# Letting ScalarE load one tile of neighbour rows per pass, row by row, in a graph kernel whose gathers run on GpSimd

## The reference, cut to what matters

```
def _rgcn_layer(x, W, SW, b, src, dst, rel):
    xt = jnp.einsum('nd,rde->rne', x, W)
    agg = jax.ops.segment_sum(xt[rel, src], dst, num_segments=x.shape[0])
    return jax.nn.relu(agg + x @ SW + b)
...
x1 = rgcn(x, w1, sl1, b1);  x2 = rgcn(x1, w2, sl2, b2);  x = layernorm(x + x2)
feat = jax.nn.relu(x @ W1 + b1)
h = feat * d_invsqrt
agg = jax.ops.segment_sum(h[src], dst, num_segments=N)
out = layernorm(x + (feat - agg * d_invsqrt) @ W2 + b2)
```

## Time and profile before

| | |
|---|---|
| time, median of 3 runs | 6150.97 us (6150.61 to 6153.27) |
| the profiled execution's own time | 6150.52 us |
| its span, first to last instruction | 6148.7 us |
| GpSimd busy | 4639.2 us (75%) |
| TensorE busy | 3443.3 us (56%) |
| VectorE busy | 1587.8 us (26%) |
| ScalarE busy | 475.0 us (8%) |

### The profile page before, as it was taken

The page is one execution under the profiler, slowest core; times in us unless marked ns, Lnnn a source line. Parts: engine busy times, 40 slices in busy tenths (PEclk is TensorE's granted clock), DMA queues, the critical chain, the costliest instruction groups (busy, mean ns, idle before and its releaser), DMA issues.

```text
span 6148.7 us, 76649 instructions
## 1 busy us (share of the span) xinstructions
PE 3443.3 (56%) x13474; PEld 2442.4 (40%) x13626; DVE 1587.8 (26%) x2521; ACT 475.0 (8%) x1056; POOL 4639.2 (75%) x4906
## 2 busy tenths in 40 slices
PE   4666666666666666666666666674434434344344
PEld 3343333433344444344343434353333333333333
DVE  5433333433344222122221222231111111111111
ACT  1000000000010111011110101010000000000000
POOL 7777777777777777777777777777777777777776
PEclk8776776777676767777667676775555555555555
DMA  2222222222222222222222222222222222121222
GB/s 78 63 58 61 64 58 61 57 64 61 57 61 63 60 64 67 67 67 61 74 60 67 67 65 69 68 66 59 60 57 60 60 60 60 57 64 56 60 60 60
DMA packets 220298, 384.36 MB, mean 63 GB/s; under 512 B 96977, under 2 KB 117196, under 8 KB 220108
## 3 DMA queue, kind: packets, MB, share of 16 engines
q0 software_dynamic: 156672, 321.18, 18.3%
q1 hardware_dynamic: 61766, 60.62, 3.1%
q10 hardware_dynamic: 1670, 0.85, 0.0%
HBM read 356.54 MB, written 25.73 MB: 62 GB/s over the span
## 4 chain that ended last, share of the span: by engine, by line
POOL 72%; issue 25%; PE 2%; POOLq 0%; DVE 0%; DMA 0%; ACT 0%; DVEq 0%; ACTq 0%; SPq 0%
POOL rows L804 72%; PE bank L961 1%; PE bank L989 1%; POOL rows L786 0%; POOLq L812 0%; POOLq L797 0%; DMA rows<-in_x_dram,idx 0%; DVE acc L1071 0%; PE bank L1382 0%; POOLq L106 0%; PE bank L1303 0%; ACT r_agg L924 0%; PE bank L1511 0%; DMA rows<-h_d,idx 0%; PE bank L1296 0%
## 5 line engine op out<-in xcount | busy, mean ns | idle before, releaser
L804 POOL DMA_INDIRECT rows<-in_x_dram,idx x1632 | 1545.9, 947 | 499.9 <-issue 496.5
L804 POOL DMA_INDIRECT rows<-h_d,idx x1611 | 1531.1, 950 | 491.2 <-issue 490.9
L804 POOL DMA_INDIRECT rows<-x_d,idx x1618 | 1527.9, 944 | 493.5 <-issue 493.5
L989 PE MATMUL bank<-r_S,rows 128*128 128x128 f32 x6644 | 1230.3, 359 | 972.6 <-DMA rows<-x_d,idx 453.2
L989 PEld LDWEIGHTS bank<-r_S,rows 128*128 128x128 f32 x6644 | 1155.4, 266 | 1052.2 <-issue 1040.1
L1164 PE MATMUL bank<-r_S,rows 128*128 128x64 f32 x3322 | 767.7, 424 | 1138.7 <-DMA rows<-h_d,idx 1122.7
L1164 PEld LDWEIGHTS bank<-r_S,rows 128*128 128x128 f32 x3322 | 726.2, 331 | 1182.7 <-DMA rows<-h_d,idx 674.0
L1027 DVE TENSOR_TENSOR r_S<-bank,key 128x1792 f32<-128x1792 f32 x238 | 480.3, 2018 | 932.2 <-PE bank L989 927.3
L924 ACT COPY r_agg<-bank 128x512 f32<-128x512 f32 x476 | 278.5, 585 | 2491.3 <-PE bank L989 2472.7
L1208 DVE TENSOR_TENSOR acc<-acc,bank 128x64 f32 x238 | 52.8, 222 | 1613.3 <-PE bank L1164 1597.5
L961 PE MATMUL bank<-r_agg,w1s 128*128 128x512 f32 (+1 forms) x512 | 447.7, 1043 | 25.9 <-ACT r_agg L924 25.9
(11 more groups left out here) (157 smaller groups left out, 1317.8 us busy)
## 6 DMA issues: line engine op xcount, KB each, us to landing
rows<-in_x_dram SPq DMA_DIRECT2D x3712, 0.5 KB
rows<-x_d SPq DMA_DIRECT2D x3712, 0.5 KB
rows<-h_d SPq DMA_DIRECT2D x3712, 0.5 KB
rows<-in_x_dram,idx POOLq DMA_INDIRECT x1632, 2.5
rows<-x_d,idx POOLq DMA_INDIRECT x1618, 2.5
rows<-h_d,idx POOLq DMA_INDIRECT x1611, 2.5
d_xr<-in_x_dram SPq DMA_DIRECT2D x48, 256.0 KB, 2.9
x_d<-d_yr SPq DMA_DIRECT2D x24, 256.0 KB, 3.1
```

The source lines that it names most:

```text
L804: pool.indirect_dma_start(out=self.c.rows[:, self.place(s), :], out_offset=None, in_=self.table[:, :], in_offset=bass.IndirectOffsetOnAxis ...
L989: mm = pe.matmul(agg_ps[j][:, bass.ds(offs[j * KG + k], TK)], c.rows[:, g.place(h * KG + k), :], S[:, pb, j * KG + k, :], start=False, sto ...
```

## The change

A second tile of every full pass leaves GpSimd, which gathers 54: `OWN = (UN - 2, UN - 1)`. Both own tiles are the last of group 7; SyncE now loads tile 54 (`BY_SYNC`), ScalarE tile 55 (`BY_ACT`). ScalarE loads its tile with the same `load_own`, in eight lists of 16 rows: three at once at the end of a pass (`own_next`, behind the last copy and `take`, ahead of the chunk's tail), one at the start of the next pass ahead of the first copy, and one behind each of the copies of groups 0 to 3 (in layer 3: two behind each of the first two `take`s). It fetches its next list of addresses after the eighth. At the start of a layer `own_first` issues the first three lists ahead of the tail's first `d_xT`. Semaphores are shared (`node_src_out`, `lo_hi_rel_out`, `yzf_turned`, `zf_copied`, `fv_mm` and others), which makes room for the new ones; the waits stay, with other counts.

```
-OWN = UN - 1
+OWN = (UN - 2, UN - 1)
+BY_SYNC, BY_ACT = range(2)
 LIST = 16
+LISTS = P // LIST
+AT_ONCE = 3
+assert LISTS == AT_ONCE + 1 + 4
...
-                        if s < skip or (part is FULL and s == OWN):
+                        if s < skip or (part is FULL and s in OWN):
                             continue
...
+    def fetch_list(self, eng, o, i):
+        eng.dma_start(self.c.list_i[o][0:1, :], self.c.own_d[bass.ds(i, 1), o, :]).then_inc(self.list_in[o], 16)
+    def own_free(self, eng, o, q, i):
+        eng.wait_ge(self.summed, self.pairs_summed(q, i, OWN[o] // PT))
+        self.list_there(eng, o, q, i)
+        gate(eng, self.c.passed)
+    def load_own(self, nc, eng, o, lists):
+        for first in [n * LIST for n in lists]:
+            _, starts = nc.values_load_multi_w_load_instructions(
+                c.list_i[o][0:1, first:first + LIST], engines=bass.OrderedEngineSet([eng.engine]), ...)
+            for row, start in enumerate(starts, first):
+                eng.dma_start(to[row:row + 1, :], table[bass.ds(start, ROW)].unsqueeze(0)
+                              ).then_inc(self.own[o][row // (P // OWN_SEMS)], 16)
...
 # layers 1 and 2, ScalarE
         with act.Fori(0, rounds) as q:
+            own_first(nc, act, c, g, q)
             def iteration(i, part):
+                if part is FULL:
+                    g.load_own(nc, act, BY_ACT, [AT_ONCE])
                 act.wait_ge(mixed, q * NIT + i + 1)
                 for h in range(...):
                     act.wait_ge(summed, ...)
                     act.copy(agg[:, h, :, :], ...)
                     if part is FULL and h % PAIR == PAIR - 1:
                         g.take(act, h // PAIR, q, i + 1)
+                    if part is FULL and AT_ONCE + 1 + h < LISTS:
+                        g.load_own(nc, act, BY_ACT, [AT_ONCE + 1 + h])
+                        if AT_ONCE + 2 + h == LISTS:
+                            g.fetch_list(act, BY_ACT, i + 1)
+                if part is FULL:
+                    own_next(nc, act, g, q, i)
             by_chunk(act, c, q, iteration, tail.act_early, tail.act_late)
...
+def own_first(nc, act, c, g, q):
+    act.wait_ge(g.cleared, q + 1)
+    gate(act, c.passed)
+    g.fetch_list(act, BY_ACT, 0)
+    g.own_free(act, BY_ACT, q, 0)
+    g.load_own(nc, act, BY_ACT, range(AT_ONCE))
+def own_next(nc, act, g, q, i):
+    with act.If(i < IT - 1):
+        g.own_free(act, BY_ACT, q, i + 1)
+        g.load_own(nc, act, BY_ACT, range(AT_ONCE))
+    act.end_ifs()
...
 # layer 3, ScalarE
                 if part is FULL:
+                    g.load_own(nc, act, BY_ACT, [AT_ONCE])
                     for p in range(PR):
                         g.take(act, p, q, i + 1)
+                        if p < PR // 2:
+                            g.load_own(nc, act, BY_ACT, [AT_ONCE + 1 + 2 * p, AT_ONCE + 2 + 2 * p])
+                        if p == PR // 2 - 1:
+                            g.fetch_list(act, BY_ACT, i + 1)
+                    own_next(nc, act, g, q, i)
```

More of the change, by code:

```diff
@@ L150, in build @@
         c.gs8 = sb("gs8", [1, NG])
-        c.list_i = sb("list_i", [1, P], I32)
+        c.list_i = [sb(f"list_i{o}", [1, P], I32) for o in range(len(OWN))]
         c.step_t, c.step_g, c.carry = sb("step_t", [P, 1]), sb("step_g", [P, 1]), sb("carry", [P, 1])
@@ L730, in __init__ @@
         assert [s.num - self.landed[0].num for s in self.landed] == list(range(RING + PAIR))
-        self.own = [sem(f"own{b}") for b in range(OWN_SEMS)]
-        assert [s.num - self.landed[-1].num for s in self.own] == list(range(1, OWN_SEMS + 1))
-        self.list_in = sem("list_in")
+        self.own = [[sem(f"own{o}_{b}") for b in range(OWN_SEMS)] for o in range(len(OWN))]
+        assert [s.num - self.landed[-1].num for own in self.own for s in own] == list(range(1, len(OWN) * OWN_SEMS + 1))
+        self.list_in = [sem(f"list_in{o}") for o in range(len(OWN))]
         self.cleared = sem("cleared")
@@ L829, in run @@
                 pool.dma_reset(landed)
-                pool.sem_clear(range(self.landed[0].num, self.own[-1].num + 1))
+                pool.sem_clear(range(self.landed[0].num, self.own[-1][-1].num + 1))
                 pool.sem_inc(self.cleared, 1)
@@ L835, in run @@
             self.early(pool, rounds, stored)
-    def load_own(self, nc, sync, q, i):
-        c = self.c
[L840 to L844, removed]
-        for first in range(0, P, LIST):
+    def fetch_list(self, eng, o, i):
+        eng.dma_start(self.c.list_i[o][0:1, :], self.c.own_d[bass.ds(i, 1), o, :]).then_inc(self.list_in[o], 16)
@@ new lines, in own_free, with list_there @@
+    def own_free(self, eng, o, q, i):
+        eng.wait_ge(self.summed, self.pairs_summed(q, i, OWN[o] // PT))
+        self.list_there(eng, o, q, i)
+        gate(eng, self.c.passed)
+    def list_there(self, eng, o, q, i):
+        eng.wait_ge(self.list_in[o], q * ((IT + o) * 16) + i * 16 + 16)
+    def load_own(self, nc, eng, o, lists):
+        c = self.c
+        to, table = c.rows[:, self.place(OWN[o]), :].bitcast(U8), self.table.bitcast(U8).rearrange("n b -> (n b)")
+        for first in [n * LIST for n in lists]:
@@ L846, in load_own @@
             _, starts = nc.values_load_multi_w_load_instructions(
-                c.list_i[0:1, first:first + LIST], engines=bass.OrderedEngineSet([sync.engine]),
+                c.list_i[o][0:1, first:first + LIST], engines=bass.OrderedEngineSet([eng.engine]),
                 min_val=0, max_val=(N - 1) * ROW, skip_runtime_bounds_check_because="nodes of the graph")
-            for j, start in enumerate(starts):
-                sync.dma_start(to[first + j:first + j + 1, :], table[bass.ds(start, ROW)].unsqueeze(0)).then_inc(self.own[(first + j) // (P // OWN_SEMS)], 16)
+            for row, start in enumerate(starts, first):
+                eng.dma_start(to[row:row + 1, :], table[bass.ds(start, ROW)].unsqueeze(0)
+                              ).then_inc(self.own[o][row // (P // OWN_SEMS)], 16)
@@ L852, in wait_rows @@
     def wait_rows(self, pe, part, h, i, k):
         tiles, half = part.of(h), halves(part, h)
-        if part is FULL and h == OWN // KG:
+        if part is FULL and h == RING - 1:
+            gathered = KG - len(OWN)
             if k == 0:
-                pe.wait_ge(self.landed[h], i * ((KG - 1) * 16) + (KG - 1) * 16)
-            if k == OWN % KG:
-                for own in self.own:
+                pe.wait_ge(self.landed[h], i * (gathered * 16) + gathered * 16)
+            if h * KG + k in OWN:
+                for own in self.own[k - gathered]:
@@ L1254, in reach, with rows_of @@
         def reach(k):
-            passes_to(sync, c, k, lambda i, part: g.load_own(nc, sync, q, i))
+            def rows_of(i, part):
+                g.fetch_list(sync, BY_SYNC, i)
+                g.own_free(sync, BY_SYNC, q, i)
+                g.load_own(nc, sync, BY_SYNC, range(LISTS))
+            passes_to(sync, c, k, rows_of)
         def finish(ch):
@@ L1593, in dve_late @@
         for ch in chunks:
[L1594 to L1595 removed]
+            dve.wait_ge(self.yzf_turned, ch.m * 3 + 3)
+            dve.wait_ge(self.dinv_moved, 48)
             dve.wait_ge(self.stored, ch.free)
```

145 lines of the change are left out of this document (73 added, 72 removed).

## The result

The changed kernel takes **6184.75 us** (median of 4 runs, 6182.28 to 6191.86) against 6150.79 for the kernel before on the same chip: ratio 1.0057, interval 1.0039 to 1.0074. It is 0.6% slower; forecast were 6192 and 0.7%. One gather fewer in each of 87 passes, and the launch is 34 us longer.

A forecast was written before the change was run, and what follows sets the result against it. GpSimd's gathers were taken to bound the kernel, 55 a step of 68.7 us. Layers 1, 2 and 3 at -19, +92 and -32 gave +41 us on 6150.5: 6192 us, forecast range 6100 to 6350, eight in ten 6055 to 6750.

The forecast's parts named there:

- ScalarE becomes the pacer of layer 2: Layer 2: lists between copies delay TensorE's groups 6 and 7; steps with a tail 72.3 us against 68.7, +49 us.
- rival A: All layers: everything hides, through cheaper lists on ScalarE or TensorE catching up faster; 6062 us, chance 0.24.
- The wait for the generator: SyncE and ScalarE issuing DMAs at once: 0.3 us more a list, counting only in layer 2, +31 us.
- rival B: Descriptor generator taken for the whole DMA, lists of 8.0 us while SyncE issues; 6750 us; chance 0.26 including what lies between.
- Layer 1: Layer 1's sum: -36 us from its steps and +17 from its start, -19 in all.
- the step's 67.5: Layer 1: GpSimd's 54 gathers still set the step at 67.5 us; ScalarE and TensorE finish at 65.1, 2.4 left.
- The stall at the start: Start of layer 1: first lists delay the first `take` to 94.5 us, GpSimd waits until 94.9, +17 us.
- the loop's registers: ScalarE's step before the fourth list: register loads and the branches around them, estimated at about 1.9 us.
- The way into layer 2: Start of layer 2: lists ahead of the tail make the first pass end 11.5 us later, +12 us.
- Layer 3: Layer 3's sum: -36 us from steps under 67.5, +4 from its start, -32 in all.
- late first `take`: Start of layer 3: first `take` at 4159.6 us, the gather needing it due at 4155.51, +4 us.
- The prediction's own lower end: Whole kernel: no waits for the generator and a faster TensorE group would give 6125 us.

The follow-up runs named there:

- e11: Changed kernel, but layer 1 with nine lists on SyncE and seven on ScalarE, layer 2 with none on ScalarE; 6096.55 us, ratio 0.9916 to the kernel before.
- e2: Changed kernel, but SyncE loads no rows, ScalarE alone loads tile 55, GpSimd gathers 55 in all layers; 9769.71 us beside 9761.21, ratio 1.0007.
- e12: Changed kernel with 64 extra semaphore increments in ScalarE's program ahead of its first layer; 6253.95 us, ratio 1.0174 to the kernel before.
- e10: The same kernel as e11, an earlier run on another chip at the slow pace; 9753.73 us beside 9680.28 for the kernel before.

## Why the prediction was right, step by step

**ScalarE becomes the pacer of layer 2: right, and nearly to the microsecond.** Forecast for copies 0 to 4, at t = 37.8, 44.4, 51.2, 57.7, 65.0; the step shown has 37.8, 44.5, 51.6, 58.2, 65.4. What was off is the end: groups 6 and 7 with their gaps take 5.6 us and not 6.7, because the second of them runs in 1.72 us, the value that the prediction gave to rival A. The step is 71.6 in place of 72.3; steps without a tail 61.5 (62 forecast). The steps cost +43 us (1962 against 1919) where +49 was said. e11 confirms the place: without ScalarE's lists in layer 2 its steps sum to 1919 again.

**The wait for the generator: mis-sized, +31 for nothing.** Row DMAs of 0.222 median on ScalarE and 0.225 on SyncE, SyncE's rows 0.326 us apart on average within a list before and after: two engines issuing at once cost nothing measurable. Of the two rules weighed in the prediction, the exclusive lock of the Trainium skill's "Perfetto Trace Analysis", section "DMA Instruction — HWDGE (DVE, Sync)", has no price here at 0.22 us a DMA, and rival B is out. The estimate had been made from ScalarE's first DMA of the launch, 0.64 us. The first row of each of ScalarE's lists shows 0.46 as well, and the rows behind it 0.22 beside the same SyncE; in e2, where SyncE issues no rows, the first shows the same 0.46. Dear is the first of a series, not the company.

**Layer 1: -19 forecast, +12 measured; the term that failed is the step's 67.5.** The stall at the start was right (GpSimd waits 17.5 us in place of 17, its gather at 94.55, forecast 94.9). But the steps with a tail are 68.2, set by ScalarE: copy 0 comes at t = 32.9 and not 30.6, which is the branch's pause, and from there to copy 4 it is 28.3 us and not 27.1. The forecast had 2.4 us of slack and the two took all of it. The 28 steps add up to 1897.2 us; 28 of 67.5 would be 1890. The other 24 of the 31 us are the late start itself: TensorE's first pass ends late, and in e12 its next eight steps make that good (516.7 us in place of 540), which a ScalarE that needs 68.2 doesn't allow. e12 shows what the instructions cost: with the branch's pause and the gaps gone the step needs 65.0, the forecast's 65.1, and layer 1 ends at 1992.1, -14.4 against before (e11 -18.6). That is the -19 of the forecast, less the longer stall at the layer's start (GpSimd waits 21.6 us there in place of 17.5, for the 64 increments). The prediction had priced "the loop's registers" at 1.9 and never asked whether the loop's code is still there when the branch is taken, though SyncE's branch showed the price in the trace of before.

**The way into layer 2: +12 forecast, +12.8 measured.** **Layer 3: -32 forecast, -36 measured.** Read as the prediction does at the `take`s it is +17 for the start and -53 for the steps, since GpSimd runs ahead of TensorE's late first pass and the steps then catch up. Read at GpSimd it is simple: from its first gather for this layer to the end are 6180.7 - 4154.8 = 2025.9 us, before 6148.7 - 4087.1 = 2061.6. The 4 us forecast for the late first `take` didn't come.

**The sum.** +12, +13, +43, -36: +32, against +41. Two terms were wrong and of opposite sign, the generator (+31 that wasn't there) and layer 1 (31 too good), so the total is closer than its parts, and that it came within 8 us is luck. The prediction's own lower end, 6125, had two conditions, no wait for the generator and a faster group; both came true, and the kernel took 6185. Of rival A one part was true, the faster group; that all hides was not.

By the Trainium skill, "Runtime: NRT & Kernel Launch", section "Instruction fetch mechanics", an engine other than TensorE holds 512 instructions in two pages of 256, and a branch to a target outside them waits for a DMA. The traces agree in this: each row is two instructions, so 128 rows alone are 256 in a pass, and ScalarE's trace has 324, 327 and 305 from one L698 branch to the next in the three layers, where it had 53, 54 and 34. A loop of 325 lies in two such pages or in three, depending on where it starts; that is what 64 instructions ahead of it would change. By that rule this change had a term of its own, which the prediction left out. The size of the pages is not shown: what the traces have is the gap at every 128th instruction and packets of 8.2 KB on q14 (3.58 MB in 437), and where the edges lie was not tried.

## What to carry to other kernels

Unrolled register-addressed DMAs cost twice: their issue time on a sequencer whose busy share says nothing, and the length of the loop's code; count instructions per iteration before and after, and look in the trace at the gap behind the loop's branch, on every engine and before the change too: in the runs here loops of up to 98 instructions on ScalarE, VectorE and SyncE never paid, and of those of 272 to 335 some did and some did not. Place such work layer by layer, where the slack of the engine that gets it is larger than the work: seven lists in layer 1, none in layer 2, eight in layer 3 turned 0.6% slower into 0.8% faster here. When an engine is relieved, compute first how far the next one is from its own limit, with what stands ahead of its work: on SyncE that was the wait behind the stores, a branch of 2.5 us and 3.6 us of address fetch.

## What the runs showed of the hardware

**Code position is worth over 1%.** The changed kernel and e12 do the same work; 64 instructions ahead of a loop move 2.4 us a branch between layers and make 6185 into 6254 (1.0057 and 1.0174 of the kernel before, each on its own chip).

**Rows can be issued at a third of the pace while GpSimd gathers.** On four occasions, on chips where the kernel before took 9680 to 9773 us, gathers had their usual 0.94 us and 1.25 period, but SyncE's rows didn't (SyncE's timeline of e10, then GpSimd's):

```profile
3800.23 44.48 SPq L869 DMA_DIRECT2D rows<-x_d  x42
...
3876.78 23.29 SPq L869 DMA_DIRECT2D rows<-x_d  x60
```

```profile
3868.75 0.95 POOL L812 DMA_INDIRECT rows<-x_d,idx  x1 [0.30 <-issue]
3897.80 0.94 POOL L812 DMA_INDIRECT rows<-x_d,idx  x1 [28.11 <-ACT idx L776]
```

While GpSimd gathers, 42 rows take 44.5 us, 1.06 each; while it waits (3869.7 to 3897.8), 60 take 23.3, 0.39 each. Over the whole of e10, register loads included, it is about 1.1 us a row beside gathers and 0.44 without for SyncE, about 0.9 and 0.45 to 0.5 for ScalarE; at the usual pace it is 0.40 beside gathers, where nearly all rows lie. The rows then take longer than the step. e2, which issues as many rows a pass as the kernel before, took as long as it did (1.0007); the kernels with more rows took 0.6 to 11% longer. One chip showed both behaviours at different times, so it isn't fixed to a chip. What causes it stays open.
